# A graph network on one Trainium2 core: the edges' target one-hots of the opening move to ScalarE, with one copy deferred and two waits renamed

## What is computed

```python
z = jnp.einsum('ni,hif->nhf', h, W)                 # h: the layer-normed x
el = jnp.einsum('nhf,hf->nh', z, a_l)
er = jnp.einsum('nhf,hf->nh', z, a_r)
e = jax.nn.leaky_relu(el[src] + er[dst], NEG_SLOPE)
...
out = jax.ops.segment_sum(alpha[:, :, None] * z[src], dst, num_segments=N)
```

## Time and profile before

| | |
|---|---|
| median of 3 runs | 2652.1 us (2650.57 to 2652.84) |
| the profiled execution | 2653.19 us, span 2651.4 us |
| PE busy | 2512.2 us, 95% of the span |
| DVE busy | 1914.7 us, 72% |
| ACT busy | 1144.2 us, 43% |
| granted TensorE clock, mean | 0.974 |

### The profile page before, as it was taken

The page is one execution under the profiler, slowest core; times in us unless marked ns, Lnnn a source line. Parts: engine busy times, 40 slices in busy tenths (PEclk is TensorE's granted clock), DMA queues, the critical chain, the costliest instruction groups (busy, mean ns, idle before and its releaser), DMA issues. The chain is left out here.

```text
span 2651.4 us, 34230 instructions
## 1 busy us (share of the span) xinstructions
PE 2512.2 (95%) x12453; PEld 1694.3 (64%) x12453; DVE 1914.7 (72%) x2412; ACT 1144.2 (43%) x1344; POOL 128.1 (5%) x151
## 2 busy tenths in 40 slices
PE   6999379969999999999999999999999899998998
PEld 4666268846666666666666666666666566587776
DVE  7876778888987887887798788788878543454111
ACT  5322366565455455555545545555553222121111
POOL 0000000010000000000000000000000000000222
PEclk9999689979999999999999999999999999999999
DMA  5211410053223222222321422222240002025996
GB/s 161 61 33 38 90 58 1 1 169 94 55 53 80 71 62 56 72 60 56 94 55 40 93 63 58 68 71 62 55 118 32 8 12 58 20 63 213 319 334 192
DMA packets 173575, 218.49 MB, mean 82 GB/s; under 512 B 66648, under 2 KB 116442, under 8 KB 173430
## 3 DMA queue, kind: packets, MB, share of 16 engines
q1 hardware_dynamic: 163570, 197.85, 27.3%
q0 software_dynamic: 4928, 10.25, 1.5%
q10 hardware_dynamic: 4932, 8.30, 0.9%
HBM read 187.23 MB, written 32.56 MB: 83 GB/s over the span
## 5 line engine op out<-in xcount | busy, mean ns | idle before, releaser
L1651 PE MATMUL wide_ps<-keep_own_w1g,rails_hid_hi 128*125 128x512 f16 x2120 | 632.5, 380 | 2.9 <-DVE rails_hid_lo L1368 2.9
L1651 PE MATMUL wide_ps<-keep_own_w,rails_hid_hi 128*125 128x512 f16 x2080 | 618.9, 379 | 3.2 <-issue 3.2
L1651 PE MATMUL wide_ps<-keep_own_w1g,rails_hid_lo 128*125 128x512 f16 x1060 | 402.7, 380 | 0.0
L1651 PE MATMUL wide_ps<-keep_own_w,rails_hid_lo 128*125 128x512 f16 x1040 | 394.2, 379 | 0.0
L1651 PEld LDWEIGHTS wide_ps<-keep_own_w1g,rails_hid_hi 128*125 128x125 f16 x2120 | 285.6, 137 | 157.7 <-issue 4.5
L1651 PEld LDWEIGHTS wide_ps<-keep_own_w,rails_hid_hi 128*125 128x125 f16 x2080 | 279.3, 136 | 156.0 <-issue 4.6
L1143 ACT ACTIVATE rails_hid_hi<-rails_raw_a,keep_scale_hidden 128x1000 f16<-128x1000 f32 x210 | 274.2, 1334 | 209.3 <-DVE rails_raw_a L1387 91.9
L1368 DVE SCALAR_TENSOR_TENSOR rails_hid_lo<-rails_raw_a,keep_scale_hidden,rails_hid_hi 128x1000 f16<-128x1000 f32 x210 | 312.1, 1516 | 43.8 <-ACT rails_hid_hi L1143 43.7
L1133 ACT ACTIVATE rails_raw_a<-wide_ps,keep_scale_gelu 128x1000 f32<-128x1000 f32 (+1 forms) x192 | 181.7, 952 | 324.0 <-PE wide_ps L1636 320.9
L1422 DVE SCALAR_TENSOR_TENSOR keep_X<-wide_ps,rails_out_scale,keep_X 125x1024 f32<-125x1024 f32 x180 | 198.6, 1103 | 131.7 <-PE wide_ps L1651 131.6
L1651 PEld LDWEIGHTS wide_ps<-keep_own_w1g,rails_hid_lo 128*125 128x125 f16 x1060 | 145.1, 137 | 84.6 <-issue 0.8
(11 more groups left out here) (414 smaller groups left out, 3543.1 us busy)
## 6 DMA issues: line engine op xcount, KB each, us to landing
carried_w_land<-cproj SPq DMA_DIRECT2D x79, 1024.0 KB
ffn_w<-W SPq DMA_DIRECT2D x51, 1024.0 KB, 13.1
rails_xs<-xt_d SPq DMA_DIRECT2D x124, 78.1 KB
xt_d<-rails_acc SPq DMA_DIRECT2D x20, 250.0 KB, 4.2
keep_X<-x SPq DMA_DIRECT2D x10, 448.0 KB
z_d<-open_z SPq DMA_DIRECT2D x10, 448.0 KB
att_zh<-z_d SPq DMA_DIRECT2D x4, 1120.0 KB
xn_d<-ffn_xn SPq DMA_DIRECT2D x10, 448.0 KB
```

The lines of the kernel that those rows point to most:

```text
L1651: mm = nc.tensor.matmul(ps[0:P, t, :], hid[(q + b) % 2][l][:, k, t * P:(t + 1) * P], w[(q + b) % 2][r][:, k, :], start=(k == 0 and i == 0) ...
```

## The change

From tile 1 on ACT makes the target one-hots, in groups of four: it takes the absolute difference of a node number and the edge's target into a new tile `apart` (four buffers), and then Relu(1 - difference), which is 1 where the difference is 0 and 0 elsewhere. DVE makes the source one-hots, and in tile 0 both. `hot_ready` becomes `src_ready` and `dst_ready`, and PE waits for both. ACT reads the bounds per tile. The second half of z is copied not at the end of its own tile but in the next one, after `x_hi`, and `comb_hi` moves with it from tile 1 to tile 2. Ahead of `w_sum` ACT counts `apart_set` up by the chunks of tile 0 in a loop.

```diff
+        apart = [c.sb(f"apart{k}", [P, P], F16) for k in range(GROUP)]
...
                             nc.vector.tensor_scalar(hot_src[k][:], iota_h[:], src_f[:, bass.ds((first + g) * GROUP + k, 1)],
-                                                    None, ALU.is_equal)
-                            nc.vector.tensor_scalar(hot_dst[k][:], iota_h[:, t * P:(t + 1) * P],
-                                                    dst_f[:, bass.ds((first + g) * GROUP + k, 1)], None,
-                                                    ALU.is_equal).then_inc(hot_ready, 1)
+                                                    None, ALU.is_equal).then_inc(src_ready, 1)
+                            if t == 0:
+                                nc.vector.tensor_scalar(hot_dst[k][:], iota_h[:, 0:P],
+                                                        dst_f[:, bass.ds((first + g) * GROUP + k, 1)], None,
+                                                        ALU.is_equal).then_inc(dst_ready, 1)
...
+                dve.sem_inc(dst_ready, 1)
                 dve.wait_ge(bounds_out, 1)
...
-                            pe.wait_ge(hot_ready, done + g * GROUP + (k + 1))
+                            pe.wait_ge(src_ready, done + g * GROUP + (k + 1))
+                            pe.wait_ge(dst_ready, done + g * GROUP + (k + 2))
...
+                def dst_hots(t):
+                    first, groups, done = load_bounds(act, t)
+                    with act.Fori(0, groups) as g:
+                        act.wait_ge(dst_ready, done + g * GROUP + 1)
+                        for k in range(GROUP):
+                            nc.scalar.activation(apart[k][:], iota_h[:, t * P:(t + 1) * P], ACT.Abs,
+                                                 bias=dst_f[:, bass.ds((first + g) * GROUP + k, 1)], scale=-1.0).then_inc(apart_set, 1)
+                        for k in range(GROUP):
+                            act.wait_ge(apart_set, done + g * GROUP + (k + 1))
+                            act.wait_ge(hot_used, done + g * GROUP + (k + 1))
+                            nc.scalar.activation(hot_dst[k][:], apart[k][:], ACT.Relu, bias=1.0, scale=-1.0).then_inc(dst_ready, 1)
...
+                act.wait_ge(bounds_out, 1)
+                first, groups, done = load_bounds(act, 0)
+                with act.Fori(0, groups):
+                    act.sem_inc(apart_set, GROUP)
                 for k in range(4):
                     w_sum(k)
                 for t in range(TILES):
+                    if t >= 1:
+                        dst_hots(t)
                     act.wait_ge(counted, t + 1)
...
+                    if t >= 2:
+                        z_copy(t - 1, 1)
+                    if t == 2:
+                        act.wait_ge(scale_step, 3)
+                        nc.scalar.activation(combs["hi"][:].rearrange("p o h f -> p (o h f)"), comb.rearrange("p o f -> p (o f)"),
+                                             ACT.Copy, scale=up_scale[:, 0:1].bitcast(F32)).then_inc(hi_set, 1)
                     z_copy(t, 0)
                     if t == 0:
                         z_copy(t, 1)
                     count_turned(t)
-                    if t >= 1:
-                        z_copy(t, 1)
-                    if t == 1:
-                        act.wait_ge(scale_step, 3)
-                        nc.scalar.activation(combs["hi"][:].rearrange("p o h f -> p (o h f)"), comb.rearrange("p o f -> p (o f)"),
-                                             ACT.Copy, scale=up_scale[:, 0:1].bitcast(F32)).then_inc(hi_set, 1)
+                z_copy(TILES - 1, 1)
```

More of the change, by code:

```diff
@@ L161, in opening @@
         scale_step, hi_set, lo_set = c.sem("scale_step"), c.sem("hi_set"), c.sem("lo_set")
-        hot_ready, hot_used = c.sem("hot_ready"), c.sem("hot_used")
+        src_ready, dst_ready, apart_set, hot_used = c.sem("src_ready"), c.sem("dst_ready"), c.sem("apart_set"), c.sem("hot_used")
         counted, f_ready, u_ready = c.sem("counted"), c.sem("f_ready"), c.sem("u_ready")
```

## The result

The changed kernel takes 2657.99 us, the median of 7 runs (2656.66 to 2661.58), against 2650.57 for the kernel before in 7 runs beside it (2647.97 to 2652.84). The ratio is 1.0028 with a 95% interval of 1.0016 to 1.0040: 7.4 us slower, a small change clear of the noise. The forecast was +7.7 us.

A forecast was written before the change was run, and what follows sets the result against it. PE was taken to set the opening's pace, losing time where DVE feeds its loops. Loops -4.8, late starts +4.3 and +4.5, tile 2 -0.15 and clock +3.8 summed to +7.7 us, 2659.8, range 2649.5 to 2669.

The forecast's parts named there:

- The loops' gain: Counting loops of tiles 1 to 9 get shorter with target one-hots on ACT: -4.8 us together.
- The pace: In the counting loops ACT sets the pace at 2.27 us per group of four, between PE's 2.08 and DVE's old 2.47.
- a hand-over: Between groups, ACT's next first Abs waits for dst_ready of the current group: taken as 0.16 us.
- Tile 1's late start: PE starts tile 1's loop late, waiting for ACT's count_turned, exposed register loads and first one-hots: +4.3 us.
- Tile 4's late start: Deferred z copy delays x's tiles 6 to 9, then the statistics and tile 4's one-hots: +4.5 us (3 to 6).
- 10.4 us: Time from issue of tile 2's z store to the end of traffic from loading x's tiles 6 to 9.
- The clock: PE's pauses ahead of tile 1's and tile 4's loops drop its clock to 1.2 GHz: +1.9 us each, +3.8 (0 to 3.8).
- Tile 2: Start of tile 2's loop: DVE is the later engine and saves one target one-hot, -0.15 us.
- Tile 0: ACT's bound loads and register-count loop come behind tile 0's eight spreads: taken as nothing, at most +2.3 us.
- a clock that doesn't fall: Rival: no or short clock fall in tiles 1 and 4, so +3.9 us, 2656.0; chance 0.22.
- an ACT bound at 2.94 or 2.5 per group: Rival: ACT bounds the loops, 2.94 us per group without overlap (2684) or 2.5 (2668); chance 0.15.
- ACT keeps up: Rival: ACT's group stays under 2.08 us, PE runs at 0.521 per chunk in every loop, 2649; chance 0.12.

The follow-up runs named there:

- e6_fill: The changed kernel with PE adding zero products 8 times more ahead of tile 1's loop and 12 times more ahead of tile 4's: 2654.48 us, ratio 1.0019.
- e4_defer_only: The kernel before plus only the deferral (z's second half copied next tile, comb_hi in tile 2), all one-hots on DVE: 2658.21 us, ratio 1.0032.
- e7_no_abs: The changed kernel without the Abs, Relu reading zero-filled apart tiles, so only times count: 2653.65 us in one run; tile 3's loop 10.57 us.
- e8_split: e3_both with DVE making every fourth target one-hot from tile 2 on: 2641.82 us, ratio 0.9969.
- e2_x_early: The changed kernel with SP issuing the loads of x's tiles 6 to 9 ahead of its wait for tile 2's z: 2650.14 us, ratio 0.9996.
- e9_counts_later: The changed kernel with SP storing tile 3's counts only once x's last tile has landed: 2659.6 us in one run, against 2650.74 before.
- e5_no_defer: The changed kernel with the deferral undone, so ACT copies z's second half in its own tile before the target one-hots: 2682.76 us, ratio 1.0126.
- e3_both: The changed kernel with tile 1's target one-hots back on DVE and x's tiles 6 to 9 loaded before tile 2's z store: 2644.17 us, ratio 0.9976.

## Why the prediction was right, point by point

- **The loops' gain** was put at -4.8 us. The table gives -1.29 in tile 2, -0.45 in tiles 3, 5, 7 and 8 each, -0.71 in tile 6, -0.24 in tile 9, and with the clock's part removed by e6_fill 10.97 - 12.21 = -1.24 in tile 1 and 10.95 - 12.22 = -1.27 in tile 4: -6.6. (Tile 1's 12.21 isn't fixed: without any change to that loop it was 11.46 in e4_defer_only.) The pace was right (2.27 foreseen, 2.21 to 2.24 seen; e7_no_abs and e8_split show that it is ACT's). The loops came out 0.2 us shorter because the price of a group was put too high: in tile 3 a step between groups takes (11.01 - 2.07)/4 = 2.24 us on average (2.07 is the last group, from 120.97 to 123.04), which over the 36 steps gives about 1.1 of the 1.8 us, with the late loops of tiles 1, 2 and 4 a little shorter still (2.21 to 2.23 a step) and some rounding for the rest. That the first two groups ran at PE's pace gives nothing, for the third began 4.49 us into the loop, twice 2.24. Relus start each 0.20 us and one takes 0.294, where I had 0.215 and 0.309 from L707; that and a hand-over of 0.14 to 0.19 make the 2.21 to 2.24. The Trainium skill (ScalarE: Activation LUTs, What ACT_TABLE_LOAD costs) gives 186 ns plus 0.833 ns per column and 93 ns of overlap, by which an estimate is 0.197 and 0.290: the trace agrees. By those figures a group is 0.07 us shorter than mine and the sum 2.6, for the 0.05 and 1.9 in the prediction left out the last Relu.
- **Tile 1's late start**: +4.3 foreseen, +4.6 measured; the register loads showed 0.81 us instead of the 0.5 that I had put.
- **Tile 4's late start**: +4.5 foreseen, +6.3 measured, outside the 3 to 6 that I gave it. The chain was right (e2_x_early and e4_defer_only show it); the term that was mis-sized is "10.4 us" from the store's issue to the last load. It was 12.2. In the kernel before nobody waited for these loads, so its trace shows no landing; but it shows traffic up to 120.0 to 120.5, and I had read its end as 119.25 (see e9_counts_later).
- **The clock**: +3.8 foreseen, 1.6 + 2.1 = 3.7 measured by e6_fill. That it came so close is in part luck. I had put 5.3 us of work at half clock in each loop; the granted clock was back at 1.00 3.3 us into tile 1's loop and 4.5 into tile 4's (the slices 65 to 66 and 147 to 148 above), but the loops were shorter at full clock than I had reckoned.
- **Tile 2** -0.1, and no wait for z's store: as foreseen. **Tile 0** +0.1: on ACT the first `w_sum` follows the last weight spread without a gap, so the bounds are read under the spreads. The 0.1 itself means nothing, as tile 1's opening matmuls come anywhere from 55.5 to 58.0 us in the five traces with the same tile 0 (the changed kernel, e2, e5, e6 and e9).

The sum, -6.6 + 4.6 + 6.3 + 3.7 with the small ones, is +8.0 at the end of the opening; two terms were off by about 1.8 us each in opposite directions. The mechanism was right, but that the sum came within 0.3 us of the measured 7.4 is luck, and the interval of that measurement reaches from 4.2 to 10.6. The rival of a clock that doesn't fall is out, and so is that of an ACT bound at 2.94 or 2.5 per group. The rival in which ACT keeps up is the one that an edit brings about: e8_split is that kernel.

Per one-hot ACT is the dearer engine here, 0.29 + 0.20 against 0.167 us. That did not decide: e3_both has the one-hots of tiles 2 to 9 on ACT and is 6.2 us faster than before, since ACT had the time and DVE had not. The rule of the Trainium skill that operations such as relu belong on VectorE (ScalarE: Activation LUTs, Rules for kernel authors) agrees with the trace on the price, and not with e3_both on the outcome.

## What to carry to other kernels

When a step is deferred, follow every instruction queued behind its semaphore on every queue: here the copy of z was free, and four loads that SP listed behind it cost more than the change could gain. When work moves to an idle engine, ask not how idle it is but when its last task ahead of the new one ends; the loop's first chunk is paid at that time, and a pause of PE at that place can be paid a second time in clock. And where two engines can both make the parts, divide them so that each stays under the consumer's pace.

## What the runs showed that I had not expected

Pauses of equal length did not cost the same clock. In e5_no_defer the first chunk came the same 3.9 us after the opening matmuls in each of tiles 3 to 9, with 3.4 us between PE's weight loads. In tiles 3, 4 and 7 the loop then took 12.5 us; in tiles 5 and 8 (10.96) and in tiles 6 and 9 (13.17 and 8.72) it was as short as at full clock. The granted clock behind two of these pauses, tile 3's and tile 5's, PE alone (start:end, length, busy, clock, DMA share, GB/s):

```profile
124.00:126.00 2.00, 2.00 (x8) 0.50 1.01 252
...
181.00:184.00 3.00, 3.00 (x19) 1.00 0.00 0
```

In tile 3 the fall came after work had been taken up again at 122.49, and lasted past 126; in tiles 4 and 7 it came just before the first chunk. So a pause of this length may or may not halve the clock (what decides it, no run here shows), while those of 4.8 and 6.8 us between weight loads in the changed kernel did so before their end.
